# Gated cross attention with a slot memory: the output rows are stored in quarters of their columns in place of halves

## What is computed

```python
Q = layernorm(x) @ Wq.T + bq;  K = ctx @ Wk.T + bk
x = x + tanh(g_xattn) * softmax(Q @ K.T / sqrt(2048)) @ ctx

h = layernorm(x)
query = h @ fWq.T                                   # 64 wide
scores = (query @ Wr.T) @ (aux_keys @ Wr.T).T / sqrt(48) + log_rel      # 512 slots, top 8 kept
w = softmax over the 8 kept slots
aux = (w @ aux_values[kept]) @ Wvd.T @ Wvu.T        # 128 wide in between
gate = function of the variance of h and of gelu(h @ Wu1.T + bu1) @ Wu2.T + bu2
x = x + tanh(g_ffn) * (h + gate * aux)
```

## Time and profile before

| | before |
|---|---|
| median of 3 timed runs | 1056.72 us |
| time of the profiled execution | 1057.0 us |
| span of the profiled execution, first to last instruction | 1054.9 us |
| TensorE busy | 1029.0 us, 98% of the span |
| VectorE busy | 741.0 us, 70% |
| ScalarE busy | 562.2 us, 53% |
| granted TensorE clock, mean | 0.995 |

### The profile page before, as it was taken

The page is one execution under the profiler, slowest core; times in us unless marked ns, Lnnn a source line. Parts: engine busy times, 40 slices in busy tenths (PEclk is TensorE's granted clock), DMA queues, the critical chain, the costliest instruction groups (busy, mean ns, idle before and its releaser), DMA issues.

```text
span 1054.9 us, 19143 instructions
## 1 busy us (share of the span) xinstructions
PE 1029.0 (98%) x6730; PEld 983.6 (93%) x6730; DVE 741.0 (70%) x1863; ACT 562.2 (53%) x884; POOL 170.7 (16%) x357
## 2 busy tenths in 40 slices
PE   6999999998999999999999999999999997999998
PEld 5999999998999999999999999999999996788886
DVE  3888557466747676767767676776767666888886
ACT  3654777546536454454645445464554554555553
POOL 0000000000012322223232222322222233000000
PEclk9999999999999999999999999999999998999999
DMA  7976656789389955753545835357463549999998
GB/s 227 213 166 189 249 201 244 277 311 286 75 238 234 239 141 142 178 138 101 117 122 135 201 80 136 102 116 208 104 147 80 131 149 336 359 351 406 404 422 352
DMA packets 258373, 219.02 MB, mean 208 GB/s; under 512 B 220564, under 2 KB 232884, under 8 KB 244664
## 3 DMA queue, kind: packets, MB, share of 16 engines
q1 hardware_dynamic: 248536, 180.68, 60.1%
q10 hardware_dynamic: 9216, 33.56, 8.0%
q0 software_dynamic: 576, 4.19, 1.0%
HBM read 174.10 MB, written 54.79 MB: 217 GB/s over the span
## 4 chain that ended last, share of the span: by engine, by line
PE 87%; DVE 5%; DMA 3%; DVEq 2%; issue 1%; ACT 1%; SPq 0%; ACTq 0%
PE tk_bank L59 23%; PE tk_bank L61 23%; PE tk_bank L60 23%; PE tk_bank L1898 3%; PE tk_bank L1900 3%; PE tk_bank L1243 2%; PE tk_bank L106 2%; DVE tk_bank L407 1%; PE tk_bank L1227 1%; PE tk_bank L1228 1%; PE tk_bank L1234 1%; DVE a_T L391 1%; DVEq L403 1%; DMA k_rows<-in_Wk_dram 1%; DMA b_weights<-scratch_b 1%
## 5 line engine op out<-in xcount | busy, mean ns | idle before, releaser
L59 PE MATMUL tk_bank<-b_weights,k_turned 128*128 128x384 f32 (+2 forms) x1056 | 348.0, 330 | 1.8 <-DVE b_weights L945 1.4
L60 PE MATMUL tk_bank<-b_weights,k_turned 128*128 128x384 f32 (+2 forms) x1056 | 339.4, 321 | 0.0
L61 PE MATMUL tk_bank<-b_weights,k_turned 128*128 128x384 f32 (+2 forms) x1056 | 339.3, 321 | 0.0
L59 PEld LDWEIGHTS tk_bank<-b_weights,k_turned 128*128 128x128 f32 x1056 | 199.0, 188 | 5.5 <-DVE b_weights L945 1.6
L60 PEld LDWEIGHTS tk_bank<-b_weights,k_turned 128*128 128x128 f32 x1056 | 199.2, 189 | 1.5
L61 PEld LDWEIGHTS tk_bank<-b_weights,k_turned 128*128 128x128 f32 x1056 | 198.7, 188 | 0.0
L1345 ACT ACTIVATE k_turned<-tk_bank 128x512 fp32r<-128x512 f32 x124 | 70.6, 595 | 50.8 <-DVE tk_bank L1561 50.8
L1561 DVE STREAM_TRANSPOSE tk_bank<-k_rows 128x512 f32<-128x512 f32 x128 | 87.6, 709 | 9.4 <-DMA k_rows<-in_x_dram 9.1
L1374 ACT ACTIVATE k_rows<-tk_bank 128x512 f32<-128x512 f32 x31 | 18.5, 598 | 117.0 <-PE tk_bank L1234 117.0
L1569 DVE TENSOR_TENSOR k_turned<-tk_bank,k_turned 128x512 fp32r<-128x512 f32 x124 | 79.8, 685 | 0.9
L59 PE MATMUL tk_bank<-k_turned,a_T 128*128 128x256 f32 x256 | 73.6, 288 | 1.8 <-DVE a_T L391 1.2
(11 more groups left out here) (300 smaller groups left out, 2304.5 us busy)
## 6 DMA issues: line engine op xcount, KB each, us to landing
k_rows<-in_x_dram SPq DMA_DIRECT2D x32, 1024.0 KB, 4.8
k_rows<-in_x_dram SPq DMA_DIRECT2D x128, 256.0 KB, 4.5
late_x<-in_x_dram SPq DMA_DIRECT2D x18, 1024.0 KB, 9.5
out_dram<-late_x ACTq DMA_DIRECT2D x36, 512.0 KB, 13.8
k_rows<-in_Wq_dram SPq DMA_DIRECT2D x16, 1024.0 KB, 4.9
early_x<-in_x_dram SPq DMA_DIRECT2D x14, 1024.0 KB, 8.1
out_dram<-early_x ACTq DMA_DIRECT2D x28, 512.0 KB, 12.9
k_rows<-in_Wk_dram SPq DMA_DIRECT2D x40, 256.0 KB, 5.1
```

Of the source, the lines that this page charges most:

```text
L59: pe.matmul(out, lh, rh, start=start, stop=False, skip_group_check=skip)
L60: pe.matmul(out, lh, rl, start=False, stop=False, skip_group_check=skip)
L61: return pe.matmul(out, ll, rh, start=False, stop=stop, skip_group_check=skip)
```

## The change

`store` issues two DMAs where it issued one, each for a quarter of the columns (`QN` = 512), each behind its own wait for the add of that quarter. The counts that the ring's semaphores are waited for go from 32 to 64 for a tile, since each DMA raises its semaphore by 16.

```diff
@@ sync @@
-            sp.wait_ge(stored[t % RING], 32 * (t // RING))
+            sp.wait_ge(stored[t % RING], 64 * (t // RING))
@@ scalar @@
         def store(t, s, half):
-            cols = slice(half * D // 2, (half + 1) * D // 2)
-            act.wait_ge(S["added"], 4 * t + 2 * half + 2)
-            act.dma_start(xout[t][:, cols], x[s][:, cols]).then_inc(stored[s], 16)
+            for n in (2 * half, 2 * half + 1):
+                cols = slice(n * QN, (n + 1) * QN)
+                act.wait_ge(S["added"], 4 * t + n + 1)
+                act.dma_start(xout[t][:, cols], x[s][:, cols]).then_inc(stored[s], 16)
@@ scalar, at the end @@
-            act.wait_ge(stored[s], 32 * len(range(s, TILES, RING)))
+            act.wait_ge(stored[s], 64 * len(range(s, TILES, RING)))
```

## The result

The changed kernel takes 1068.38 us, the median of 6 runs (1066.12 to 1070.3); the kernel before takes 1057.22 us beside it (6 runs, 1056.32 to 1058.2). The ratio is 1.0109, interval 1.0097 to 1.0121: slower by about 11.2 us, where 1057.9 us was forecast. The profiled execution took 1068.95 us, with a span of 1066.8 us.

A forecast was written before the change was run, and what follows sets the result against it. PE was taken to set the output stage's pace, with the DMA engines full too. ACT 0, loads 0 and DMA 4.3 - 3.06 = +1.2 us gave 1057.9 us against the 1056.7 us median; range 1056.0 to 1062.5 us.

The forecast's parts named there:

- What ACT's list costs: Output stage on ACT: 64 added issues of 0.34 us each fit into gaps; 0, other end 1.0 us.
- Rival 2: Output stage: ACT's queue holds issues, delaying `affine`, DVE and PE; sign: issues above 0.8 us; +3.4 us, 1060.1 us; chance 0.20.
- Loads: Loads waiting for their buffer's stores: the tightest found has 12.8 us of slack, so none comes late; 0.
- The DMA work: Output-stage stores: 49 half tiles at 0.087 us more, 4.3 us, less 3.06 us of DMA idle time: +1.2 us.
- rival 1: End of the output stage: only the tail counts, small packets' extra work (2.3%) vanishes in idle time; 1056.1 us; chance 0.20.
- Rival 3: Queued stores: 2 KB packets cost 97 ns; +10.6 us, 1067 us; chance 0.17, including any packet cost giving over 2.1 us.
- The tail: Last store: 256 KB in place of 512 KB, 0.64 us less, already inside the 3.06 us of DMA idle time.

The follow-up runs named there:

- 12: Kernel before, with half-tile stores issued by SP and the late loads by GpSimd, as early as before, none by ACT: 1061.72 us, ratio 1.0046.
- 13: Changed kernel's quarter stores issued by SP, late loads by GpSimd, none by ACT, against the kernel before: 1063.58 us, ratio 1.007.
- 9: Kernel before, with half-tile stores issued by SP and loads by ACT four tiles ahead: 1062.7 us, ratio 1.0047.
- 10: Changed kernel's quarter stores issued by SP, loads by ACT four tiles ahead, against the kernel before: 1068.47 us, ratio 1.01.
- 1: Kernel before, with quarter stores in the last tile alone: 1056.89 us, ratio 0.9996; the last 256 KB land 2.6 us after their issue.
- 3: Changed kernel's quarter stores issued by SP, loads by ACT five tiles ahead, against the kernel before: 1064.22 us, ratio 1.0079.
- 4: Kernel before, with half-tile stores issued by SP and loads by ACT five tiles ahead: 1061.0 us, ratio 1.0034.
- experiment 5: Separate program of stores alone, back to back on ACT, in series of one shape each, computation left out: 512 KB issues held 1.25 us, 256 KB 0.66 us.
- experiment 14: Separate program: ACT stores halves, quarters, then spaced halves while SP loads 12 tiles, computation left out; halves held 3.2 us, quarters mostly 2.5 to 2.7, spaced halves never.
- experiment 7: Changed kernel's quarter stores, with `affine` of the next tile ahead of them in ACT's list, against the kernel before: 1067.44 us, ratio 1.0093.

## Why the prediction was wrong

- **The step that failed** is "What ACT's list costs": it priced 64 added issues at 0.34 us each, found a gap for every one and put 0 into the sum (0 at both ends for a common tile, 1.0 us at most for three others). The gaps are there (the median issue is 0.34 us, and the quarters make nothing late up to tile 14), but an issue's length isn't a constant: 18 of the 128 took over 1 us, up to 4.46, and ACT's `affine` and `hi` behind them came late. The term at 0 measured 8.5 us of idle time on PE and 1.4 us of lower clock behind it.
- **The rival was right, its price wrong.** Rival 2 named the cause, the direction (78 packets becoming 156 against a limit between), the waits and even the signs that show it. It had a chance of 0.20 and a price of 3.4 us (1064.5 us in its longer form), since it let the stage fall back only to the DMA engines' pace. Its count was too high (65 measured for its 78, 90 for its 156), and its limit in packets isn't borne out: the longest holds began at 52 and 53. The holds come in bursts instead: two in a row ahead of one `affine` delay it by 7.6 us, two more delay `hi`, PE stops for 6.4, and then the clock takes 1.4 us more. The DMA engines work on through the stop, so the queue is shorter behind it (median landing 9.4 us in place of 17.1), and they are idle at the end, at a share of 0.53: PE's time was lost, theirs can't buy it back.
- **Loads were fine.** No load is late in the changed kernel; `affine`'s long waits are all for its own queue or for DVE.
- **The DMA work was undersized.** The page gives ACT's queue 8.7% of 16 engines' span in place of 8.0%. That is 92.8 - 84.4 = 8.4 us per engine (7.4 to 9.5 by rounding), 0.13 us a half tile in place of my 0.087:
```profile
q10 hardware_dynamic: 18432, 33.56, 8.7%
...
q10 hardware_dynamic: 9216, 33.56, 8.0%
```
  (The first row is of after, the second of before.) The 2 KB packet has a median of 84 ns, as I took, but a mean of 90, and the 4 KB one 164; sums go by means. 49 x 0.13 - 3.06 = +3.3 us would have been my forecast without holds: the size that 12 and 13 (+1.9) and 9 and 10 (+5.1 to 5.8, where all 64 half tiles count and the engines are full at the end) bracket. Of a half tile's 1.287 us, 0.13 is 10%, so rival 1's 2.3% is far too low. Rival 3's 97 ns was too high. The fixed 2.0 us that it quotes from the Trainium skill, "DMA: Bandwidth & Descriptors", stand there in the section "Anatomy of one DMA — SWDGE (gpsimd) path", as a fit for DMAs that GpSimd issues and not for ACT's.
- **The tail** brought 0.1 to 0.2 us (1 and the changed kernel's own last landing, 2.5 for 2.7), not 0.64: it was priced by packets alone.
- **Together:** in the changed kernel all of the delay comes through PE, and PE's waits through ACT's held issues; the DMA engines are half idle at the end, so their added work costs only by making the queue longer. What quarters cost where no compute stands behind their issues is 1.9 us (12 and 13), 3.2 (3 and 4) or 5.8 (9 and 10). That leaves some 5 to 9 of the 11.2 us to the compute that stands behind held issues on ACT. This is a difference between kernels that also differ in other ways, not a reading of one trace.
- **Open** is what decides that an issue is held. It isn't the mean count of packets in flight alone: the longest holds began at 52 and 53, and an issue of 0.34 us at 83. One of the 16 engines may have been behind the others, which a mean doesn't show; the size of the packets, the pairing of two stores within 0.5 us and the loads beside them are other candidates that no run here separates. The early holds of experiment 5 and the pace of its 8 KB series are open too.

## What to carry to other kernels

Don't price a DMA issue as a constant when the engine that issues it also computes. Before splitting a transfer into smaller rows on such a queue, count what will be in flight (issues per us x landing time x packets each), in packets and not in DMAs. A count above what the trace has shown without a hold (65 here) is a warning. It isn't a limit to trust: after the first burst, this kernel was held below it. What a hold costs is read from the list: everything behind the issue waits, and two or four holds in a row add up before the next compute instruction. Finer stores gain nothing while a transfer's landing time is mostly fixed or the queue stands. If small rows are needed, issue them from an engine that has nothing else to do, and look at the longest issue in the trace, not the median.

## What the runs showed of the chip

- Beside loads, back-to-back issues on ACT took some 0.5 us each until about 80 packets per engine were in flight, and then 3.2 us for 512 KB and 2.5 to 2.7 us for 256 KB (experiment 14). With the loads over they took 0.85 us at some 100 packets.
- In the kernels issues were held for up to 5.6 us on ACT (experiment 7; 4.46 in the changed kernel) and 7.1 us on SP (13). In the changed kernel the first of over 1 us came when the count had reached 90, the longest began at 53. In kernels with stores on SP, 4 KB packets were held too, up to 3.41 us (9). 14 DMAs in flight with 64 packets cost at most 1.2 us an issue, 7 DMAs with 94 packets up to 5.5.
- Without loads issues back to back are held at the engines' pace: 1.25 us for 512 KB from the third or fourth on, 0.66 us for 256 KB from the sixth on.
- In a queue a 2 KB store packet takes 84 ns at the median and 90 at the mean, two of them some 15 ns more than a 4 KB one (164 ns mean).
- A 256 KB store with nothing ahead lands after 2.5 us, a 512 KB one after 2.7.
- The issue of a DMA of 64 rows takes 0.55 us, of 128 rows 0.34 us.
